# A two-layer graph network on one Trainium2 core: the first step's threshold guess is made without squares, and work is reordered at the heads of both steps

## What is computed

```python
R = S / S.sum(axis=1)                     # S = adj + identity
Xf, Xa = X, X
for s in range(2):
    logits = (Xa @ W1) @ W2 @ (Xa @ W3).T # 2048 x 2048
    # softmax of each row; keep the largest entries until their sum reaches 0.9; softmax again
    A = adj_from_feats(Xa)
    Xf = R @ Xf                           # diffusion
    Xa = A @ Xa                           # attention
    Z = Z + (Xf @ U1[s] + Xa @ U2[s])
return x + layernorm(X + Z)
```

## Time and profile before

| | |
|---|---|
| median of 3 runs | 1416.79 us (1416.27 to 1417.39) |
| the profiled execution | 1413.95 us, its span 1412.2 us |
| PE busy | 1211.1 us (86%) |
| DVE busy | 1091.7 us (77%) |
| ACT busy | 613.0 us (43%) |
| POOL busy | 273.7 us (19%) |
| mean granted TensorE clock | 0.942 |

### The profile page before, as it was taken

The page is one execution under the profiler, slowest core; times in us unless marked ns, Lnnn a source line. Parts: engine busy times, 40 slices in busy tenths (PEclk is TensorE's granted clock), DMA queues, the critical chain, the costliest instruction groups (busy, mean ns, idle before and its releaser), DMA issues.

```text
span 1412.2 us, 17981 instructions
## 1 busy us (share of the span) xinstructions
PE 1211.1 (86%) x6042; PEld 589.8 (42%) x6042; DVE 1091.7 (77%) x1863; ACT 613.0 (43%) x1164; POOL 273.7 (19%) x236
## 2 busy tenths in 40 slices
PE   0669999989797998999997998879899679999692
PEld 0224555543243454454453553334444334454351
DVE  7997777714999599799899102899379999999868
ACT  1634554537422564564442336540374254241130
POOL 7033332220422031031121001311001011111011
PEclk9989999998999999999998999999999889999896
DMA  7045665521344001001002003344312201512165
GB/s 238 39 166 197 206 219 188 173 105 49 104 135 134 1 31 62 14 31 47 30 30 75 6 25 119 112 175 152 106 30 82 83 16 53 162 40 68 52 228 175
DMA packets 56310, 139.73 MB, mean 99 GB/s; under 512 B 9568, under 2 KB 9568, under 8 KB 52128
## 3 DMA queue, kind: packets, MB, share of 16 engines
q1 hardware_dynamic: 56224, 138.71, 29.2%
HBM read 88.62 MB, written 50.07 MB: 98 GB/s over the span
## 4 chain that ended last, share of the span: by engine, by line
PE 42%; DVE 28%; issue 12%; ACT 9%; DMA 4%; POOL 3%; SPq 1%; DVEq 1%; POOLq 0%; ACTq 0%
DVE WS L1430 10%; PE UB L701 6%; PE RB L863 3%; PE AB L863 3%; PE AB L691 3%; PE AB L684 3%; PE XB L701 3%; ACT E L1118 3%; PE RB L701 3%; DVE w L1644 3%; PE RB L808 2%; PE TB L710 2%; POOL RT L591 2%; DMA AD<-xu_d 2%; PE AB L808 2%
## 5 line engine op out<-in xcount | busy, mean ns | idle before, releaser
L1430 DVE SCALAR_TENSOR_TENSOR WS<-E,g 128x2048 bf16<-128x2048 f32 x128 | 315.1, 2512 | 28.2 <-ACT E L1118 27.1
L1513 DVE TENSOR_REDUCE g<-E 128x1 f32<-128x2048 f32 x32 | 73.0, 2281 | 113.1 <-ACT E L1091 112.9
L1160 ACT ACTIVATE turns<-TB 128x512 f16<-128x512 f32 x128 | 75.7, 594 | 148.9 <-PE TB L716 148.7
L710 PE MATMUL TB<-ident,E 128*128 128x128 f32 x512 | 83.7, 293 | 41.2 <-DVEq L1704 29.3
L591 POOL TENSOR_TENSOR RT<-RT,AD 128x512 f32<-128x512 f32 x32 | 54.0, 1688 | 293.7 <-ACT RT L1130 293.6
L710 PEld LDWEIGHTS TB<-ident,E 128*128 128x128 f32 x512 | 67.5, 151 | 67.4 <-DVEq L1704 31.7
L1154 ACT ACTIVATE turns<-TB 128x512 f16<-128x512 f32 x128 | 75.6, 594 | 39.0 <-PE TB L710 38.9
L1607 DVE SCALAR_TENSOR_TENSOR E<-E,g 128x2048 f32<-128x2048 f32 x33 | 80.2, 2461 | 12.8 <-issue 12.6
L1091 ACT ACTIVATE E<-LB 128x512 f32<-128x512 f32 x128 | 75.5, 598 | 22.2 <-PE LB L783 20.5
L606 POOL TENSOR_TENSOR XHL<-WF,XHL 128x512 f16<-128x512 f32 x16 | 25.6, 1601 | 292.9 <-ACT XHL L1175 292.9
L716 PE MATMUL TB<-turns,minus_e 128*128 128x512 f16 x128 | 52.0, 410 | 33.4 <-ACT turns L1154 33.4
(11 more groups left out here) (309 smaller groups left out, 2428.8 us busy)
## 6 DMA issues: line engine op xcount, KB each, us to landing
turns<-adj_parts SPq DMA_DIRECT2D x48, 512.0 KB, 3.8
E<-adjT SPq DMA_DIRECT2D x16, 1024.0 KB, 7.6
adj_parts<-turns SPq DMA_DIRECT2D x16, 1024.0 KB, 5.2
AH<-adj_parts SPq DMA_DIRECT2D x16, 512.0 KB, 3.8
z_d<-UO SPq DMA_DIRECT2D x31, 256.0 KB, 2.3
XR<-x SPq DMA_DIRECT2D x4, 1024.0 KB, 11.9
WS<-U SPq DMA_DIRECT2D x4, 1024.0 KB, 6.1
x_d<-E SPq DMA_DIRECT2D x16, 256.0 KB, 2.0
```

Of the source, the lines that this page charges most:

```text
L710: i = mm(bank[:, k * P:(k + 1) * P], src(k), ident32[:, :], is_transpose=True, start=(k == 0), stop=(k == KC - 1), skip_group_check=True)
L1160: a(ET[:, 1, c * KC:(c + 1) * KC, :].rearrange("p b c -> p (b c)"), TB[c % 2][:, :], ACT.Copy, scale=SE).then_inc(s_et, 1)
L1430: return v.scalar_tensor_tensor(junk[t % 2], e, g4[:, k, t:t + 1], e, op, ALU.mult, accum_out=g4[:, F_, t:t + 1])
```

## The change

Five things change.

1. In the first step ACT makes no squares. `first_guess` only takes the mean; the spread of a row is worked out in `search` from `tot`, the mean and the maximum, behind the wait for the group's last exponential. The constants of the first guess and of the second pass are 1.3 in place of 1.2816 and 1.2 there.
2. `EARLY` becomes `early(g)`: 4 for groups 0 and 1, and 2 for groups 2 and 3, in both steps.
3. Where two exponentials are left for tile 0, they no longer stand together ahead of `a_out`, but one behind `e_hi(qq + 1, 0)` and one behind `e_hi(qq + 1, 1)`.
4. At the end of layer 0 (`post0_last`) and of the first step (`last_post`) the query and key product goes first on PE, ACT and POOL, the other products behind it.
5. In the second step's head the last tile of the first diffusion, `r_one(0, T - 1)`, stands ahead of `logits(s, 1)` rather than behind it.

```diff
-Z_P, PHI_P = 1.2816, 0.1755
+Z_P, PHI_P = (1.3, 1.2816), 0.1755
...
-OVERSHOOT = (1.2, 1.2)
+OVERSHOOT = (1.3, 1.2)
...
-EARLY = 2
...
+def early(g):
+
+    return G if g <= 1 else G // 2
...
             else:
                 r_one(0, T - R_LATE)
                 r_span(0, T - R_LATE + 1, T - 1)
+                r_one(0, T - 1)
                 logits(s, 1)
-                r_one(0, T - 1)
                 r_one(1, 0)
                 r_span(1, 1, R_FIRST - R_LATE)
...
+            pk_lo(T - 1, 0, T - 1, s_vl, T - 1)
             v_lo(T - 1, of(VR, T - 1))
-            pk_lo(T - 1, 0, T - 1, s_vl, T)
...
-            def post(t):
-
+            def post(t, last=False):
+
+                if last:
+                    pk_lo(t + T, 1, t, s_wl, t - OPEN)
                 pool.wait_ge(s_wf, t + 1 + OPEN)
                 pool.wait_ge(s_wh, t + 1)
                 q.tensor_tensor(XHL[:, 1, :], WF[:, :], XHL[:, 0, :], ALU.subtract).then_inc(s_wl, 1)
-                pk_lo(t + T, 1, t, s_wl, t + 1 - OPEN)
+                if not last:
+                    pk_lo(t + T, 1, t, s_wl, t + 1 - OPEN)
...
+            def post0_last(n):
+                pe.wait_ge(s_xTc, n + 1)
+                pk_product(n, XB)
+                pe.wait_ge(s_ue, n + OPEN)
+                three(UB[:, :], xh, xl, lambda k: U10p[:, k, 0, :], lambda k: U10p[:, k, 1, :]).then_inc(s_u, 1)
+                pe.wait_ge(s_ve, n + OPEN)
+                three(RB[:, :], xh, xl, lambda k: U11p[:, k, 0, :], lambda k: U11p[:, k, 1, :]).then_inc(s_v, 1)
...
             def last_post():
-                x_turned(2 * T - 1)
-                x_rest(2 * T - 1)
+                n = 2 * T - 1
+                x_turned(n)
+                x_rest(n)
+                pe.wait_ge(s_ue, n + OPEN)
+                pe.wait_ge(s_pkc, n + OPEN)
+                pe.wait_ge(s_xTc, n + 1)
+                pk_product(n, UB)
+                w_product(T - 1)
+                pe.wait_ge(s_pkc, n + 1 + OPEN)
                 u_product(T - 1)
-                w_product(T - 1)
-                p_and_k(T - 1)
...
-                    act.wait_ge(s_sq, 2 * qq + h + OPEN)
+                    act.wait_ge(s_sq, 2 * (qq - T) + h + OPEN)
...
-                for t in range(G):
-                    squared(gq * G + t, (gq % 2) * G + t)
+                if s:
+                    for t in range(G):
+                        squared(gq * G + t, (gq % 2) * G + t)
 
             def terms(s, g, tiles=range(G)):
                 gq = s * NG + g
                 for t in tiles:
                     qq, slot = gq * G + t, (gq % 2) * G + t
-                    act.wait_ge(s_sq, 2 * qq + 2 + OPEN)
+                    if s:
+                        act.wait_ge(s_sq, 2 * (qq - T) + 2 + OPEN)
...
+                split = i == 0 and g < NG - 1 and early(g + 1) < G
                 if i == 0:
                     e_lo(qq, 0)
                     e_lo(qq, 1)
@@ -1205,19 +1231,22 @@
                 e_lo(qq, 3)
                 if more:
                     e_hi(qq + 1, 0)
+                if split:
+                    terms(s, g + 1, range(G // 2, G // 2 + 1))
                 if post:
                     xT_lo(t - 1 + T)
                     post_out(t - 1)
                 if more:
                     e_lo(qq + 1, 0)
                     e_hi(qq + 1, 1)
+                if split:
+                    terms(s, g + 1, range(G // 2 + 1, G))
                 if post:
                     w_out(t - 1)
                 if ahead:
                     logits_out(qq + 2 * G, slot, (2, 3))
-                    squared(qq + 2 * G, slot)
-                if i == 0 and g < NG - 1:
-                    terms(s, g + 1, range(EARLY, G))
+                    if s:
+                        squared(qq + 2 * G, slot)
...
                     if g < NG - 1:
-                        terms(s, g + 1, range(EARLY))
+                        terms(s, g + 1, range(early(g + 1)))
                     pk(t - 1 + T, 1, t - 1, UB)
                 for j, (rs, r) in enumerate(rows):
                     r_out(rs, r, bank_of(s, g, j))
                     if s and j == 0 and g < NG - 1:
-                        terms(s, g + 1, range(EARLY))
+                        terms(s, g + 1, range(early(g + 1)))
                 if s + g == 0:
-                    terms(s, 1, range(EARLY))
+                    terms(s, 1)
...
+                pk(2 * T - 1, 1, T - 1, UB)
+                w_out(T - 1)
                 post_out(T - 1)
-                w_out(T - 1)
-                pk(2 * T - 1, 1, T - 1, UB)
...
+            def spread(ct, least):
+
+                ct(v.tensor_scalar(row(VAR), row(VAR), least, None, ALU.max))
+                ct(v.tensor_scalar(row(SIG).bitcast(I32), row(VAR).bitcast(I32), 0.5, ROOT, ALU.mult, ALU.add))
+                ct(v.reciprocal(row(A2), row(SIG)))
+                ct(v.tensor_tensor(row(A2), row(A2), row(VAR), ALU.mult))
+                ct(v.tensor_tensor(row(SIG), row(SIG), row(A2), ALU.add))
...
+                    if s == 0:
+                        return
                     ct(v.tensor_tensor(row(A1), row(MEAN), row(MEAN), ALU.mult))
-                    dve.wait_ge(s_sq, 2 * G * gq + 2 * G + OPEN)
+                    dve.wait_ge(s_sq, 2 * G * (gq - NG) + 2 * G + OPEN)
                     ct(v.tensor_reduce(row(MSQ), lq[:, sl, :], AX.X, ALU.add))
                     ct(v.scalar_tensor_tensor(row(VAR), row(MSQ), 1.0 / N, row(A1), ALU.mult, ALU.subtract))
-                    ct(v.tensor_scalar(row(VAR), row(VAR), 1e-12, None, ALU.max))
-                    ct(v.tensor_scalar(row(SIG).bitcast(I32), row(VAR).bitcast(I32), 0.5, ROOT, ALU.mult, ALU.add))
-                    ct(v.reciprocal(row(A2), row(SIG)))
-                    ct(v.tensor_tensor(row(A2), row(A2), row(VAR), ALU.mult))
-                    ct(v.tensor_tensor(row(SIG), row(SIG), row(A2), ALU.add))
+                    spread(ct, 1e-12)
...
                 if s == 0:
-                    ct(v.scalar_tensor_tensor(row(A1), row(SIG), -Z_P / 2, row(MEAN), ALU.mult, ALU.subtract))
-                    ct(v.tensor_scalar(row(LNU), row(A1), PER_E, -UNIT - 2 * LOG_N * 2.0 ** 23 + SKEW, ALU.mult, ALU.add))
-                else:
-                    ct(v.tensor_tensor(row(MEAN), row(MEAN), row(VAR), ALU.add))
-                    ct(v.scalar_tensor_tensor(row(A1), row(SIG), -Z_P / 2, row(MEAN), ALU.mult, ALU.add))
-                    ct(v.tensor_scalar(row(A1), row(A1), -FLOOR, -CAP[s], ALU.max, ALU.min))
-                    ct.free(v.tensor_scalar(row(LNU).bitcast(I32), row(A1), -PER_E / 2, UNIT, ALU.mult, ALU.add))
-                    ct(v.tensor_scalar(row(U).bitcast(I32), row(A1), PER_E / 2, UNIT, ALU.mult, ALU.add))
-                    ct(v.reciprocal(row(LNU), row(LNU)))
-                    ct(v.tensor_tensor(row(U), row(U), row(LNU), ALU.mult))
+                    return
...
-                    ct(v.scalar_tensor_tensor(row(LNU), tot[:, sl].bitcast(I32), 2.0, row(LNU), ALU.mult, ALU.add))
-                    ct(v.tensor_scalar(row(U).bitcast(I32), row(LNU), UNIT - FLOOR * PER_E, UNIT - CAP[s] * PER_E,
-                                       ALU.max, ALU.min))
+                    ct(v.tensor_scalar(row(LNU), tot[:, sl].bitcast(I32), 2.0 / PER_E,
+                                       -2.0 * (UNIT + LOG_N * 2.0 ** 23 - SKEW) / PER_E, ALU.mult, ALU.add))
+                    ct(v.scalar_tensor_tensor(row(VAR), row(MEAN), -2.0, row(LNU), ALU.mult, ALU.add))
+                    ct.free(v.tensor_tensor(row(LNU), row(LNU), row(MEAN), ALU.subtract))
+                    spread(ct, 1e-6)
+                    ct(v.scalar_tensor_tensor(row(A1), row(SIG), -Z_P[0] / 2, row(LNU), ALU.mult, ALU.add))
+                    ct(v.tensor_scalar(row(A1), row(A1), -FLOOR, -CAP[s], ALU.max, ALU.min))
+                    ct(v.tensor_scalar(row(U).bitcast(I32), row(A1), PER_E, UNIT, ALU.mult, ALU.add))
...
-                        largest(g, gq, ct, slice(0, EARLY))
-                    largest(g, gq, ct, slice(EARLY, None))
+                        largest(g, gq, ct, slice(0, G))
+                    elif early(g) < G:
+                        largest(g, gq, ct, slice(early(g), G))
                     first_guess(g, gq, ct)
                     search(g, gq, ct)
                     if g < NG - 1:
-                        largest(g + 1, gq + 1, ct, slice(0, EARLY))
+                        largest(g + 1, gq + 1, ct, slice(0, early(g + 1)))
```

24 lines of the change are left out of this document (17 added, 7 removed).

## The result

The changed kernel took **1368.98 us** (median of 4 runs, 1366.91 to 1369.29); the kernel before took 1417.09 beside it on the same chip (4 runs, 1416.27 to 1419.2). The ratio is 0.9655, with a 95% interval of 0.9638 to 0.9672: faster by 48 us, where 50.9 were forecast and 1365.9 was named. The result lies inside the range of 1352 to 1382.

What follows compares the result with a forecast made beforehand. No engine was full; PE, DVE and ACT's exponentials formed a ring whose waits bound the kernel. Terms summing to 50.9 us off the profiled 1413.95 gave 1363.1, plus 2.8 for the median 1365.9; range 1352 to 1382.

Steps and rivals of the forecast that it cites:

- A: Head of first step: waits and slow stretches go (3.3, 3.6, 5.1), four exponentials cost 4.0; 7.9 us gained.
- B: Group 0 of first step: PE's tile 0 wait, its slow stretch and the 3.05 wait for DVE go; 8.1 us gained.
- C: Group 1 of first step: split exponentials let DVE's search start at +19.8 after PE's start; 3.9 us gained.
- the ring: PE starts a group, ACT finishes next exponentials, DVE settles, PE may start the next; first-step group 1: 105.4 us, from 109.3.
- D: Group 2 of first step: exponentials move up 1.2 us at most, the longer chain costs 1.6; taken as 0.
- E: End of first step: PE's wait of 3.37 us before the second step's logits goes; 3.3 us gained.
- F: Second step's head, row tile 15 first: the 6.29 us wait and slow stretch at the first XR tile go; 8.7 gained.
- G: Group 0 of second step: waits of 3.07 with slow stretch and 10.77 go, four exponentials cost 4.0; 11.8 us gained.
- H: Group 1 of second step: earlier third maximum gives 3.3, and the 2.44 wait and slow restart go; 7.2 us gained.
- ScalarE's time was hidden: Rival, chance 0.06: only E, F and 3.27 us of A count, 15.3 in all; about 1401 us.
- A tile falls out: Rival, chance 0.04: a first-step row beyond its 8 values forces 42 passes, 99 to 160 us more; 1465 to 1526.
- the first rival: Rival, chance 0.15: moved exponentials become new waits at group starts and split places, some 16 us return; about 1382 us.

Runs made afterwards that it cites:

- u_pk: Changed kernel with the key product behind the large products again, at the end of layer 0 and of the first step: 1377.56 us.
- b_nosq: Kernel before with only the first step's squares removed and the new guess added: 1410.9 us beside 1415.25, ratio 0.9962.
- u_squares: Changed kernel with ACT's squares of the first step made again, their sums unused: 1369.9 us.
- second profile: Another profile of the unaltered changed kernel, taken in the experiments, where it was timed again at 1367.89 us.
- m_rout: Changed kernel with ACT's turned-piece copies between the halves of the diffusion tile's copy, at the first step's group starts after group 0: 1366.05 us.
- m_34: Changed kernel with three of group 1's exponentials ahead and the fourth in tile 0, in the first step alone: 1365.18 us.
- u_split: Changed kernel with the last two exponentials of groups 2 and 3 together ahead of the scaled result again: 1371.29 us.
- u_row15: Changed kernel with row tile 15 behind the logits of group 1 again, in the second step's head: 1375.83 us.
- fallback: Changed kernel with 1.1 in place of 1.3 in the first step's guess; two tiles fell out: 1751.42 us.

## Why the prediction was right, and where it was not

**A, 7.9 forecast, 9.3 and 8.7 measured** from the end of layer 0 in the two profiles. In the first, the way to the logits became 3.4 us shorter (forecast 3.3), the logits of group 0 2.7 (3.6), the row tiles behind them 5.2 (5.1), and the rest lost 2.0 (4.0). The first is shown by `u_pk`. The second is not, and here the sum came out near partly by luck: it was put down to the wait ahead of the logits, but `u_pk` and the kernel before with the first part alone have that same wait of 3.3 and took 12.7 us for the logits, not the 16.1 of the earlier trace rows. What slowed them in the profile of before stays open. The third was read rightly: the squares' removal alone takes that wait away (`b_nosq`). It is not the only thing that does, since with the squares back it is 0.88 and not 3.72, as POOL's pair was short (`u_squares`).

**DVE "just in time, with 1 us to spare"** was late: PE waited 1.63 for it. As the text said, it lay under ACT's four exponentials, and PE's total wait was 1.63 + 8.76 = 10.4, where 8.03 + 4.0 was charged: that is most of the smaller loss in A.

**B, 8.1 forecast, 8.1 measured.** The wait of 3.07 in tile 0 and its slow stretch went, and DVE was done when PE came.

**C, 3.9 forecast, 0.4 and -0.1 measured: the step that failed.** "The ring closes at 105.4" took the start of group 1 for granted once DVE was ready, and B's -3.05 for "finds it done" counted DVE's wait as gone when only its owner had changed. From 548.13 to 657.07 the ring is 108.9 us (109.4 in the second profile). Of its two parts the second was right: DVE's first pass of the search begins at

```profile
571.19 2.35 DVE L1459 SCALAR_TENSOR_TENSOR WS<-E,g 128x2048 bf16<-128x2048 f32 x1
```

and the release comes 85.9 later (forecast 85.6). The first part is 23.1 in place of 19.8. The 3.3 between them is PE's wait of 3.30 behind its first instruction, and everything in tile 0 slid by it. ACT's timeline has the reason:

```profile
551.30 0.63 ACT L1163 ACTIVATE VHL<-RT 128x512 f16<-128x512 f32 x1 [1.66 <-POOL RT L595]
551.84 1.07 ACT L1179 ACTIVATE turns<-TB 128x512 f16<-128x512 f32 x2
```

Its two exponentials ahead end at 547.5; then it copies the keys and stands 1.66 for POOL's sum before it may copy the turned piece. Before, PE's own wait for DVE covered this (0.49 was left of it). So ACT was late, and standing for POOL is the smaller part of it: `m_rout`, which puts the first copies ahead of it, leaves 2.5 of the 3.6 us and shortens the ring by 1.0 to 1.4. The rest is ACT's list ahead of these copies, the two exponentials and the key and diffusion copies; no run took that apart. In `m_34` PE starts group 1 only when ACT is almost ready too (its waits there are 0.25 and 0.29), and the ring is 105.6, what C named. That the split itself brings its 3.9 is what `u_split` shows.

**D** lost 1.1 and 0.9, inside the terms' spread. **E** came as forecast, 3.2 for 3.3.

**F, 8.7 forecast, 11.9 and 8.9 measured.** The tile itself gave its 8.7 (`u_row15`: 8.4 to 8.6 over the span). In the first profile the logits of group 0 took 11.2 us in place of 12.6 and those of group 1 14.0 in place of 15.8. The first holds in the second profile too. The second does not: there the logits of group 1 took 16.7, with a wait of 4.59 for ACT in place of 2.56. So the 3 us beyond the forecast are mostly the scatter of executions.

**G, 11.8 forecast, 11.6 and 11.4 measured**, with the wait of 8.3 met at 8.32.

**H, 7.2 forecast, 4.9 and 6.7 measured.** ACT waits for the third maximum until

```profile
1093.49 2.00 ACT L1143 ACTIVATE E<-E,nmx 128x2048 f32<-128x2048 f32 x1 [7.92 <-DVE nmx L1543]
```

19.2 us behind PE's start, but in the second profile 17.9, the very number forecast. The pair is split by two copies, and PE waits twice, 5.03 and 2.22, in place of 9.19 (3.75 and 1.95 in the second profile). The wait of 2.44 at group 2 is 2.10 in the first profile and gone in the second:

```profile
1189.34 1.04 PE L717 MATMUL TB<-ident,E 128*128 128x128 f32 x8
```

So H was sized about right, and the first profile alone would have blamed it wrongly.

**The signs of being wrong.** The prediction named two: PE waiting for DVE at group 1, which did not happen, and a wait of over 3 us behind the split exponentials. The 5.03, and the 3.75 of the second profile, are such a wait. It came in the second step, and even so the two waits there stayed under the 9.19 that they replaced. Of the signs of being right, the ring of 105 us failed and the others were met.

**The squares.** The prediction gave them no term of their own; A's 5.1 hangs on them. In the kernel before they were worth 4.3 us, in the changed kernel 1, less than the runs' spread. The 34 us of ScalarE work that went with them was mostly time that had been hidden. The four exponentials were worth 7.5, the key product 8.6 and row tile 15 6.9. These and the squares' 1 make 24 of the 48 us, with the 2.3 of the split 26. That the parts cover for each other is suggested for the squares alone (4.3 against 1); what the joint effects hold is not separated.

**The rivals.** "ScalarE's time was hidden" forecast 1401 and fell as a whole: the time is 32 us below it, and DVE waits 28.9 us less for exponentials. Of the squares by themselves it was nearly true. The rule of the Trainium skill that was set beside it, in Perfetto Trace Analysis, Identifying the Most-Contended Engine, taken alone, puts no value on relief for ScalarE at 43%, and this case does not agree: its *order* set the ring. "A tile falls out" did not happen; its price was too low, 191 us a tile where 99 to 160 were named (`fallback`): a pass takes 4.0 us and not 3.8, and the ranking behind the 42 passes was left out. The new waits of the first rival exist, 3.30, 5.03 and 2.22, but none cost much more than the wait in whose place it stood.
